# A routed expert layer on one core: one list of slots over six experts, its weighted results added to the output by accumulating scatters

## The reference, cut to what matters

```python
xn = layernorm(x)                                  # x: 6250 rows (tokens) of 256
x = x + gnn(xn, edges) + linear_attention(xn)      # the graph layer: over 80% of the time
# the part that is changed: a router and six experts, each token goes to two of them
f  = layernorm(x)
p  = softmax(relu(f @ router_w1 + router_b1) @ router_w2 + router_b2)     # over 6 experts
top_w, top_i = top_k(p, 2);  w = softmax(top_w)                           # two experts, two weights
y_e = relu(relu(f @ w1[e] + b1[e]) @ w2[e] + b2[e]) @ w3[e] + b3[e]       # 256 x 256 each
x = x + w[0] * y_{top_i[0]} + w[1] * y_{top_i[1]}
```

## Time and profile before

| | |
|---|---|
| median of 3 runs | 3523.32 us (3519.45 to 3524.82) |
| the profiled execution's own time | 3520.99 us |
| its span | 3518.9 us |
| graph layer, to the end of its last block | 0 to 2957 us |
| routing | 2957 to 3129 us |
| experts, to PE's last matmul | 3129 to 3505 us |
| PE busy, whole span | 95% |
| DVE, ACT, POOL busy | 36%, 21%, 7% |

### The profile page before, as it was taken

One profiled execution on the slowest core, in us unless ns is written; L12 is line 12 of the kernel. 1 busy time (PEld: TensorE's weight loads), 2 busy tenths in 40 slices (PEclk: granted clock), 3 DMA queues, 4 the chain that ended last, 5 costly groups with the idle time before them and its releaser, 6 DMA issues. The chain is left out here.

```text
span 3518.9 us, 49937 instructions
## 1 busy us (share of the span) xinstructions
PE 3357.5 (95%) x18034; PEld 1953.4 (56%) x18035; DVE 1279.8 (36%) x4590; ACT 736.3 (21%) x1503; POOL 258.8 (7%) x271
## 2 busy tenths in 40 slices
PE   7998999999999999999999999999999999959998
PEld 4474656566545555554555555555555555637775
DVE  7747777777711111111111111212111003544443
ACT  3445555555500000000000000000000001523332
POOL 3000000000000000000000000000000000356333
PEclk9997999999999999999999999999999999969999
DMA  7112323332389999999544447988889996248775
GB/s 205 63 47 81 145 114 125 155 155 93 135 333 303 325 318 318 328 323 310 166 150 154 151 148 258 322 284 286 281 285 307 305 303 222 69 146 281 231 257 171
DMA packets 262128, 761.09 MB, mean 216 GB/s; under 512 B 25987, under 2 KB 178492, under 8 KB 259942
## 3 DMA queue, kind: packets, MB, share of 16 engines
q1 hardware_dynamic: 169432, 613.35, 51.6%
q10 hardware_dynamic: 80910, 118.19, 12.1%
q0 software_dynamic: 11648, 27.76, 2.1%
HBM read 532.00 MB, written 239.86 MB: 219 GB/s over the span
## 5 line engine op out<-in xcount | busy, mean ns | idle before, releaser
L1540 PE MATMUL acc<-stage,split 128*128 128x448 f16 x5488 | 1045.0, 353 | 3.3 <-PEq L1491 3.3
L1540 PEld LDWEIGHTS acc<-stage,split 128*128 128x128 f16 x5488 | 537.5, 98 | 501.5 <-PEq L1491 3.5
L1540 PE MATMUL acc<-stage,other 128*128 128x448 f16 x4116 | 784.1, 353 | 0.0
L1242 PE MATMUL first_sum<-stage,other 128*128 128x448 f16 x2744 | 649.4, 354 | 0.2 <-ACT stage L1050 0.2
L1540 PEld LDWEIGHTS acc<-stage,other 128*128 128x128 f16 x4116 | 403.0, 98 | 377.9 <-issue 7.2
L1601 DVE TENSOR_TENSOR tmp<-acc,dinv_b 128x448 f32<-128x448 f32 x98 | 61.0, 622 | 1255.3 <-PE acc L1540 1255.3
L1050 ACT ACTIVATE stage<-group_ps 128x392 f16<-128x392 f32 x784 | 385.6, 497 | 296.9 <-PE group_ps L1231 293.7
L1096 DVE TENSOR_SCALAR place<-iota_col,rel 128x196 f16<-128x196 f16 x1568 | 348.2, 264 | 0.0
L1242 PEld LDWEIGHTS first_sum<-stage,other 128*128 128x128 f16 x2744 | 253.9, 98 | 139.3 <-issue 1.3
L1093 DVE TENSOR_TENSOR lanes<-iota_two,lane_two 128x256 f16<-128x256 f16 x784 | 224.7, 287 | 85.2 <-PE group_ps L1231 70.5
L1464 ACT ACTIVATE split<-r,b_two 128x448 f32 x14 | 8.9, 634 | 1122.3 <-issue 646.5
(11 more groups left out here) (347 smaller groups left out, 2551.2 us busy)
## 6 DMA issues: line engine op xcount, KB each, us to landing
stage<-adj_d SPq DMA_DIRECT2D x490, 784.0 KB, 4.3
adj_d<-stage SPq DMA_DIRECT2D x14, 5488.0 KB, 17.8
row_d<-blank ACTq DMA_DIRECT2D x20, 3340.5 KB, 57.5
other<-pack_d SPq DMA_DIRECT2D x42, 898.0 KB, 5.1
part_d<-blank ACTq DMA_DIRECT2D x10, 3340.5 KB, 57.7
slot_rows<-row_d SPq DMA_DIRECT2D x42, 393.0 KB, 5.7
rin<-root_d SPq DMA_DIRECT2D x28, 448.0 KB, 7.7
slot_base<-row_d SPq DMA_DIRECT2D x21, 393.0 KB, 6.5
```

The lines of the kernel that those rows point to most:

```text
L1242: m = mm(acc[b][k][:, 0:WIN], other[:, h, half, k * P:(k + 1) * P], stage[b][:, h, :], start=(h == 0 and half == 0), stop=(h == TILES - 1 ...
L1540: m = nc.tensor.matmul(acc[b][k][:, :], src[:, h, part, k * P:(k + 1) * P], ring[:, i, r, :], start=(h == 0 and part == 0), stop=(h == TIL ...
```

## The change

Both choices go into one list over all six experts. The region of an expert now holds every token that picked it, as first or second choice, and the list has 38 slots. Nothing is read back: the kernel first writes the rows x to the output (`kept`, SP, in the routing stage, seven batches), and each slot's three tiles are added to the output by indirect DMAs that accumulate (`compute_op=ALU.add`). As two slots can hold the same token (never within one slot, whose tokens are different ones of one expert), POOL waits before a slot's first scatter until the three scatters of the slot before have landed. `part_d`, the base rows and their loads are gone, and so is the wait in the middle. The weight of a seat is found in the expert stage from the token's first expert and two weights (`prepared`). In the routing stage every batch is ranked and seated by itself (`Choice` in place of `Set`), and POOL sends both choices of batches 0 to 5 there; both choices of batch 6, 14 scatters, are left for the next block. SP waits for all 98 before the first slot's rows. The zero fill has 12 transfers.

```diff
-SLOTS = (NP + (EXPERTS - 1) * (SLOT - 1)) // SLOT
+SLOTS = (2 * NP + EXPERTS * (SLOT - 1)) // SLOT
-CHUNKS, FOLD = 20, 17
-BLANK = 2 * (EXPERTS - 1) * REGION * ROWW // (P * CHUNKS * FOLD)
+CHUNKS, FOLD = 12, 17
+BLANK = EXPERTS * REGION * ROWW // (P * CHUNKS * FOLD)
...
-        LATE_FIRST = range(SETS[3][0] * SUB, TILES)
-        LATE_SECOND = range(SETS[1][0] * SUB, TILES)
+        l_sent = sem("g_scattered")
+        LATE = range((BATCHES - 1) * SUB, TILES)
...
+                    def kept(i):
+                        lo, hi = i * SUB, min((i + 1) * SUB, TILES - 1)
+                        sp.wait_ge(l_recc, (i + 1) * SUB)
+                        sp.dma_start(out[lo * P:hi * P, :].rearrange("(j p) f -> p j f", p=P), rows[:, lo:hi, 0:D]).then_inc(l_kept, 16)
...
-                    scattered(0, 0, l_first)
-                    scattered(0, 1, l_second)
-                    scattered(1, 0, l_first)
-                    scattered(2, 0, l_first)
+                    def scattered(n):
+                        pool.wait_ge(l_idx, n + 1)
+                        pool.wait_ge(l_row, n + 1)
+                        for j in range(n * SUB, (n + 1) * SUB):
+                            for which in range(2):
+                                nc.gpsimd.indirect_dma_start(row_d[:, :], bass.IndirectOffsetOnAxis(ap=seat_of[:, j, which:which + 1], axis=0), rows[:, j, :], None).then_inc(l_sent, 16)
+                    for n in range(BATCHES - 1):
+                        scattered(n)
...
-                        if i >= 2 and closes(i - 2) is not None:
-                            ranked(closes(i - 2))
+                        if i >= 2:
+                            ranked(i - 2)
...
-    STEPS = 2 * SLOTS
+    STEPS = SLOTS
...
+        def sent(s):
+            return 16 * ST * (s // BUF + 1)
...
-                def base_in(s, b, of):
-                    at = entry(s, 2)
-                    sp.wait_ge(k_done, s * ST + ST)
-                    sp.dma_start(base[:, b, :, :], of[bass.ds(at, SLOT), :].rearrange("(t p) c -> p t c", p=P)).then_inc(k_base[b], 16)
...
-                sp.wait_ge(l_first, 16 * TILES)
+                sp.wait_ge(l_sent, 16 * 2 * TILES)
...
+                def prepared(q, b):
+                    s = q * BUF + b
+                    if not (isinstance(q, int) and q == 0):
+                        dve.wait_ge(k_sent[b], q * (16 * ST))
+                    dve.wait_ge(k_meta, s + 1)
+                    e = expert_of[:, bass.ds(s, 1)]
+                    first, second, both = (share[:, b, n, :] for n in range(3))
+                    nc.vector.scalar_tensor_tensor(first, meta[:, b, :, FIRST], e, meta[:, b, :, W1], ALU.is_equal, ALU.mult).then_inc(k_share, 1)
+                    nc.vector.scalar_tensor_tensor(second, meta[:, b, :, FIRST], e, meta[:, b, :, W2], ALU.not_equal, ALU.mult).then_inc(k_share, 1)
...
-                        nc.vector.scalar_tensor_tensor(done[:, b, t, 0:D], done[:, b, t, 0:D], base[:, b, t, WA + second:WA + second + 1], base[:, b, t, 0:D],
-                                                       ALU.mult, ALU.add).then_inc(k_done, 1)
+                        nc.vector.tensor_scalar(done[:, b, t, :], done[:, b, t, :], share[:, b, 2, t:t + 1], None, ALU.mult).then_inc(k_done, 1)
...
+                for j in late:
+                    for which in range(2):
+                        nc.gpsimd.indirect_dma_start(row_d[:, :], bass.IndirectOffsetOnAxis(ap=seat_of[:, j, which:which + 1], axis=0), tokens[:, j, :], None).then_inc(l_sent, 16)
+                for s in range(STEPS):
+                    b = s % BUF
                     pool.wait_ge(k_idx, s + 1)
+                    if s >= 1:
+                        pool.wait_ge(k_sent[(s - 1) % BUF], sent(s - 1))
                     for t in range(ST):
                         pool.wait_ge(k_done, s * ST + (BUF * ST + t + 1))
-                        nc.gpsimd.indirect_dma_start(to[:, :], bass.IndirectOffsetOnAxis(ap=idx[:, b, t:t + 1], axis=0), done[:, b, t, 0:width], None,
-                                                     bounds_check=bound, oob_is_err=False).then_inc(k_sent[b], 16)
+                        nc.gpsimd.indirect_dma_start(out[:, :], bass.IndirectOffsetOnAxis(ap=idx[:, b, t:t + 1], axis=0), done[:, b, t, :], None,
+                                                     bounds_check=N - 1, oob_is_err=False, compute_op=ALU.add).then_inc(k_sent[b], 16)
```

More of the change, by code:

```diff
@@ L2066, in _ @@
[L2066 removed]
+                            v.then(tt(seats[:, :, :], rank_ps[:, 0:SUB, :], taken[:, :].unsqueeze(1).broadcast_to([P, SUB, EXP]), ALU.add))
+                            v.done(tt(taken[:, :], taken[:, :], rank_ps[:, SUB, :], ALU.add))
+                            v.then(tt(own[:, :, :, :], ones[:, :, :, :], seats[:, :, :].unsqueeze(2).broadcast_to([P, SUB, 2, EXP]), ALU.mult))
+                            v.then(red(seat[:, :, :], own[:, :, :, :], X, ALU.add))
@@ new lines, in _ @@
+                    batch[BATCHES - 3].weights()
+                    batch[BATCHES - 3].seated()
+                    for n in range(BATCHES - 2, BATCHES):
+                        if n == BATCHES - 1:
+                            logits_in(n)
+                            batch[n].peaks()
+                        batch[n].shares()
+                        batch[n].firsts()
+                        batch[n].seconds()
+                        batch[n].picks()
+                        batch[n].weights()
+                        batch[n].seated()
```

431 lines of the change are left out of this document (167 added, 264 removed).

## The result

The changed kernel takes 3496.53 us (median of four runs, 3494.18 to 3497.87) against 3523.89 for the kernel before (3519.45 to 3524.82): a ratio of 0.9928, 95% interval 0.9915 to 0.9941. The kernel's own profiled execution took 3496.29 us, with a span of 3494.5.

What follows compares the result with a forecast made beforehand. PE was taken to bound the experts at 8.41 us per slot. 3520.99 - 33.9 + 22.8 + 2.6 = 3512.5 us profiled, 3514.8 on the median (-8.5); range 3507 to 3575, the main forecast's own 3508 to 3521.

Steps and rivals of the forecast that it cites:

- What is hidden: the zero fill, 0, at most -3.3: Graph layer: cutting zero transfers from 30 to 12 gains 0, at most 3.3 us, PE's longest idle before its main matmul.
- Both together: +2.6: Kernel's end: 1 us for lateness of the last slots and 1.6 us for a longer last landing.
- Slots, -33.9: Experts: 42 slots become 38 at 8.41 us each, and the middle step's 0.3 us goes; -33.9 us.
- The first rows come later: End of routing: SP waits for 98 scatters instead of 49 before the first rows; +22.8 us, range +19 to +27.
- The row of 42: Routing: 14 scatters each of batches 3, 4 and 5 at 1.28 us, which POOL must finish before leaving the stage.
- The accumulating scatters: Experts: POOL 0.98 us per scatter, landing 6.2 us, chain period 8.9 before sliding; no loss in the steady state.
- rival 2: Experts: an accumulating scatter's descriptors cost POOL twice as much, 1.96 us; +20 us, 3543; chance 0.10.
- Sliding: Experts: late scatters slide to where DMA is slack, landing falls towards 3.7 us, period 6.4, so the chain settles at 8.41.
- Rival 1: Experts: chained accumulating scatters become the bound if landing stays above 5.7 us; 3562 at period 9.6, 3599 at 10.6; chance 0.27.
- Rivals 3 and 4: Experts: chain only just fits, last slots late, 3520, chance 0.14. Routing: only 7 more late scatters, 3501, chance 0.04.

Runs made afterwards that it cites:

- e1: Kernel before, with ScalarE's ten zero transfers into part_d issued behind its root-projection copies; ratio 0.9975 to the kernel before, -8.6 us.
- f1: Changed kernel with 30 zero transfers again in place of 12, measured beside the unedited changed kernel; 3547.82 us, ratio 0.9926 to the kernel before.
- f2: Changed kernel unedited, measured beside the one with 30 zero transfers; 3538.78 us, ratio 0.9897 to the kernel before.
- e4: Changed kernel with plain instead of accumulating scatters at a slot's end (output is not the sum); ratio 0.9888 to the kernel before.
- a1: Changed kernel unedited, measured again where routing is longer; 3530.78 us, ratio 0.9893 to the kernel before.
- e16: Changed kernel with 0.13 MB of weights loaded per slot instead of 0.9 from the fourth slot on, all TensorE work kept; experts 328.45 us.
- e5: Changed kernel with expert layers two and three over half the hidden columns, scatters still accumulating; experts 408.7 us.
- e15: Changed kernel with layers two and three halved, accumulating scatters, and 0.13 MB of weights per slot instead of 0.9 from the fourth slot; experts 339.2 us.
- e17: Changed kernel with expert layer two alone computed over half the hidden columns, loads whole; experts 362.7 us.
- e6: Changed kernel with expert layers two and three over half the hidden columns and plain instead of accumulating scatters; experts 246.6 us.

## Why the prediction was wrong, by its own steps

**"What is hidden: the zero fill, 0, at most -3.3". This step failed.** It cost 9.0 us before and costs 0 now; the traces show 9.0 and the medians of e1 and of f1 against f2 8.6 and 9.0. That term alone is half of the 18 us by which the forecast was too high. I looked for the fill's cost in the bytes (the DMA share, and TensorE's idle time at its main matmul) and not in the engine that issues it. The earlier trace rows gave the sign: a transfer of 57.5 us, thirty of them from ScalarE's stream, ahead of a copy that TensorE needs. The row of 6.6 us stood in the same waits view as the one of 3.3 that I took as the bound.

**"Both together: +2.6" for the tail. Wrong by 4.4 us.** The tail fell by 1.8. The accumulation did lengthen it (e4's tail is 5.2 us shorter than a1's), but I had counted to the last landing, and in the kernel before the end came some 7 us behind that, with POOL's DRAIN at 3518.7; this wait is shorter after, 2.7 us behind the last scatter in place of 8.4.

**Slots, -33.9. Right:** -35.1, with 8.41 us per slot, and 38 in place of 42.

**"The first rows come later", +22.8. Right in sum (+21.5), not in its parts.** Counted from the start of routing, batch 3's scatters began at 125.3 us, not at 129.9: I had charged the additional rankings +1.5 us, and they came 4.5 us sooner. The row of 42 took 52.9 us as forecast (53.3; the 53.6 beside it is a slip, 42 x 1.28 is 53.8), and 14 late ones landed 19.0 us behind the first (20.3). Between them stood the DRAIN: 7.8 us from POOL's last to the next block's first, where I took 3.04 from the earlier trace rows by way of VectorE's end. The earlier trace rows had shown a POOLq wait of 5.55 us there; I read past it. Two errors of some 4.5 us cancelled, and that was luck.

**The accumulating scatters.** I put GpSimd's instruction at 0.98 us; it is 1.54, between that and rival 2's 1.96, so that the third scatter is issued 3.69 us after the first, not 2.7. I put the third scatter's landing at 6.2; its median is 3.8. And I left out the 0.82 us from a landing to the next issue. Sliding is what happens: the third scatter falls behind the weights' transfer, and the chain needs 3.69 + 3.85 + 0.82 = 8.36 us. The period came out as PE's, and e16 and e4 show that nothing of it is paid per slot. But there was luck in it. I took the 2.1 us of the earlier trace rows for a landing in quiet, and it was that of a scatter without rows; the floor that I worked out from it, a period of 6.4 us, is 8.2. I counted on 2 us of room for sliding, and there are 0.2.

The Trainium skill's page "DMA: Bandwidth & Descriptors" (Queues, rings and completion order) states that the semaphore increment of a DMA lands only after every earlier write of that DMA engine, across its queues. The traces agree as far as they go: with 0.13 MB of weights loaded per slot in place of 0.9, the step from third scatter to next first falls from 7.4 to 5.3 us (e5, e15) and the median landing from 4.4 to 3.8 (changed kernel, e16)., which the prediction counts for that rule, does not bear on it.

**Rival 1, the chain as the bound (0.27).** It did not come, and narrowly: 8.36 us in the slot shown, and 8.2 at best, against 8.41. Where TensorE was given less work and the chain did become the bound (e5), the slots came every 10.7 to 12.6 us, more than the 8.6 to 10.6 that I had priced. The sliding I counted on has a far side. Once a landing is so late that VectorE waits for its buffer, the weights are issued together with the third scatter and the next slot's first scatter comes 3 us later; in e5 this lasts until the weights end, in e17 it comes and goes. Rivals 3 and 4 did not come either: PE ended without lateness, and POOL's row of 42 stood as counted.

## What to carry to other kernels

Price a DMA issue on the engine that issues it. Where an engine shows hundreds of us of idle time without a wait ahead of an instruction that another engine needs, look at the issues in its stream; moving ten of them behind that instruction cost nothing here and gave 9 us. At a block's end, ask which engine's DRAIN ends last; a row of many scatters on GpSimd adds to it. Before taking a landing as the price "in quiet", see that the transfer moved its bytes. And a serial chain whose period lies just under the bound's is no slack: with work taken off TensorE the kernel got up to 80 us slower here, so a further cut in TensorE's work has to come with a shorter chain (e6 has one, though its output is not the sum).

## What the runs showed of the hardware that I had not expected

An accumulating indirect scatter of 128 rows of 1 KB holds GpSimd 1.54 us, a plain one 0.97. With nothing else under way it lands 3.7 us after its issue; one whose rows are all left out lands after 2.7 us (plain: 2.1). A DRAIN of GpSimd's sequencer ends later by 0.08 us for each scatter of the routing block and does not end sooner when GpSimd has waited for their landings. The issue of a 3340 KB transfer, with others of its kind under way, holds ScalarE's stream for some 20 us. One and the same kernel had 205.6 us of routing in the first measurement and 236 and 244 in later ones (a1, f2), with TensorE, ScalarE and VectorE idle at once for up to 13 us, and the change was worth 27 us in the first and 37 to 38 in the later ones. The chip's number does not tell the two apart.
